# Mixture layers: the experts' sums added into x by accumulating transfers from GpSimd's queue

## The reference

```
x = w_norm * (xf * rsqrt(mean(xf * xf) + EPS))
probs = softmax(x @ w_router);  w_topk, sel = top_k(probs, 4)      # 32 experts, at most 128 tokens each
y = einsum('ecf,efh->ech', silu(g) * u, w_down)                    # per expert, on its tokens
out = zeros((T, H)).at[tok].add(gath * wv[:, None])                # each token: sum over its experts
sh = sigmoid(x @ w_shared_gate) * (silu(x @ sw_gate) * (x @ sw_up) @ sw_down)
return inp + out + sh
```

## Time and profile before

| what | us |
|---|---|
| median of three runs | 2876.78 |
| lowest and highest of the three | 2868.1, 2880.69 |
| profiled execution, whole | 2868.24 |
| its span, first to last instruction | 2866.5 |
| mean granted clock of TensorE | 0.955 of full speed |

### The profile page before, as it was taken

How to read it: one execution, slowest core, us unless ns; L and a number is a source line. 1 busy time by engine, 2 the same in 40 slices (tenths; PEclk the granted TensorE clock), 3 DMA queues, 4 the chain that set the end, 5 groups by cost and what they waited for, 6 DMA issues and landing times. The chain is left out here.

```text
span 2866.5 us, 39819 instructions
## 1 busy us (share of the span) xinstructions
PE 2626.2 (92%) x14164; PEld 1258.6 (44%) x14164; DVE 1950.7 (68%) x4228; ACT 1263.9 (44%) x1908; POOL 656.0 (23%) x640
## 2 busy tenths in 40 slices
PE   4988999999999999788898997899999999898998
PEld 2442233333333332344555564344445454455665
DVE  6778888887887886487675334867767676486334
ACT  2432466556655667543221221255555556421221
POOL 1454132131231300144001441212111110000442
PEclk8996899999999999999999998799999999999999
DMA  3004331303303210000401663723334430300566
GB/s 121 1 1 104 51 52 21 56 29 46 62 17 51 52 16 1 1 1 1 156 18 42 158 146 90 132 50 54 50 68 62 62 62 2 110 34 17 127 153 174
DMA packets 162592, 175.74 MB, mean 61 GB/s; under 512 B 19090, under 2 KB 135762, under 8 KB 162258
## 3 DMA queue, kind: packets, MB, share of 16 engines
q1 hardware_dynamic: 146948, 152.57, 24.3%
q0 software_dynamic: 12416, 17.84, 3.8%
q10 hardware_dynamic: 3040, 2.88, 0.4%
HBM read 116.32 MB, written 56.13 MB: 60 GB/s over the span
## 5 line engine op out<-in xcount | busy, mean ns | idle before, releaser
L1827 DVE TENSOR_REDUCE a_mx<-a_bank 128x1 f32<-128x512 f32 (+3 forms) x1792 | 1029.1, 627 | 274.2 <-PE a_bank L1564 186.2
L1700 ACT ACTIVATE a_E<-a_bank 128x1024 f32<-128x1024 f32 (+3 forms) x896 | 795.3, 931 | 462.4 <-PE a_bank L1621 317.9
L1564 PE MATMUL a_bank<-a_KT,a_QT 96*128 96x512 bf16 (+4 forms) x1792 | 596.3, 376 | 37.0 <-DVE a_mx L1827 27.4
L1621 PE MATMUL a_bank<-a_QT,a_KT 99*128 99x512 bf16 (+4 forms) x1792 | 508.3, 359 | 4.0 <-DMA a_QT<-a_mT 1.6
L1636 PE MATMUL a_bank<-a_E,a_Vg 128*32 128x512 f32 (+3 forms) x3584 | 438.6, 561 | 0.7 <-ACT a_E L1700 0.7
L1564 PEld LDWEIGHTS a_bank<-a_KT,a_QT 96*128 96x128 bf16 (+1 forms) x1792 | 152.6, 98 | 530.9 <-DVE a_mx L1827 331.1
L1621 PEld LDWEIGHTS a_bank<-a_QT,a_KT 99*128 99x128 bf16 (+1 forms) x1792 | 170.5, 99 | 176.5 <-ACT a_E L1700 35.2
L999 ACT ACTIVATE d_silu<-d_bank 128x512 f32<-128x512 f32 x96 | 57.2, 596 | 361.2 <-PE d_bank L873 357.5
L888 PE MATMUL d_bank<-wdT,d_hT 128*128 128x256 f32 (+1 forms) x768 | 196.9, 400 | 7.5 <-DVE d_hT L1088 7.5
L466 POOL TENSOR_TENSOR f_hl<-f_hT,f_hh 128x512 f16<-128x512 f32 x96 | 111.0, 1156 | 388.4 <-ACT f_hh L485 388.4
L792 POOL DMA_INDIRECT d_xg<-normalised,d_index x64 | 67.5, 1054 | 538.2 <-issue 535.1
(11 more groups left out here) (246 smaller groups left out, 3548.8 us busy)
## 6 DMA issues: line engine op xcount, KB each, us to landing
parts<-a_parts SPq DMA_DIRECT2D x64, 384.0 KB, 2.5
a_QT<-parts SPq DMA_DIRECT2D x180, 128.0 KB, 5.9
a_KT<-parts SPq DMA_DIRECT2D x180, 128.0 KB, 9.2
d_wgu<-in_L_ffn_w_gate SPq DMA_DIRECT2D x64, 176.0 KB
d_wgu<-in_L_ffn_w_up SPq DMA_DIRECT2D x64, 176.0 KB
d_wd<-in_L_ffn_w_down SPq DMA_DIRECT2D x64, 176.0 KB
normalised<-d_xn SPq DMA_DIRECT2D x8, 1152.0 KB, 4.7
acc<-d_zero SPq DMA_DIRECT2D x2, 4224.0 KB, 15.6
```

What stands on the lines that cost most here:

```text
L1564: last = nc.tensor.matmul(out[:, 0:w], QT[0:W, h, qt * P:(qt + 1) * P], KT[0:W, h, kh * HALF:kh * HALF + w], start=True, stop=not diag)
L1621: last = nc.tensor.matmul(out, KT[:, h, kt * P:(kt + 1) * P], QT[:, h, half * HALF + c0:(half + 1) * HALF], start=True, stop=not diag)
L1700: nc.scalar.activation(E[:, u % 2, 2 * pair:2 * pair + 2, c0:HALF], bank[:, 2 * pair:2 * pair + 2, c0:HALF], ACT.Exp).then_inc(exps, 1)
L1827: nc.vector.tensor_reduce(mx[:, j, qt, kh:kh + 1], out[:, 0:w], AX.X, ALU.max).then_inc(freed_dve, 1)
```

## The change

GpSimd takes over. After its wait for all expert additions it issues, for each chunk q, one direct transfer that reads the chunk's rows of `acc` and adds them into x in SBUF (`accum_op=ADD`). It waits for `x_done` of the chunk first, and from the fifth on for the transfer four before it, since four semaphores `summed` are used in turn. At the end it waits for all eight. SyncE's fetches and VectorE's additions are gone. In `d6_` SyncE stores chunk q when `summed` says so. In `d4_` VectorE takes the statistics of chunks 0 and 1 in slots (8, 1) and (8, 2), behind the residual of the slot. TensorE's and ScalarE's instructions are the same as before.

```diff
-    finishes = {slots[n]: qs for n, qs in ((len(slots) - 7, (0, 1)), (len(slots) - 6, (2,)), (len(slots) - 5, (3,)),
-                                           (len(slots) - 4, (4,)), (len(slots) - 3, (5,)), (len(slots) - 2, (6,)), (len(slots) - 1, (7,)))}
+    measured = {slots[len(slots) - 4 + q]: q for q in range(TPB // CT)}
...
-                sp.wait_ge(added, 16 * NE)
-                for q in range(ROWS):
-                    fetch(q)
-                for q in range(NCH):
-                    if final:
-                        sp.wait_ge(finished, START + q + 1)
+                if final:
+                    for q in range(NCH):
+                        sp.wait_ge(summed[q % SUMS], 16 * (q // SUMS + 1))
                         sp.dma_start(rows_of(dram["out"], q), core.x[:, q * CT:(q + 1) * CT, :]).then_inc(sent, 16)
-                    if q + ROWS < NCH:
-                        fetch(q + ROWS)
...
+                def sum_up(q):
+                    pool.wait_ge(x_done, START + (q + 1) * CT)
+                    if q >= SUMS:
+                        pool.wait_ge(summed[q % SUMS], 16 * (q // SUMS))
+                    nc.gpsimd.dma_start(core.x[:, q * CT:(q + 1) * CT, :], rows_of(acc, q), accum_op=ALU.add).then_inc(summed[q % SUMS], 16)
...
                 pool.wait_ge(added, 16 * NE)
+                for q in range(NCH):
+                    sum_up(q)
+                for q in range(SUMS):
+                    pool.wait_ge(summed[q], 16 * (NCH // SUMS))
...
-                def finish(q):
-
-                    tiles = core.x[:, q * CT:(q + 1) * CT, :]
-                    dve.wait_ge(back[q % ROWS], START + 16 * (q // ROWS + 1))
-                    dve.wait_ge(x_done, START + (q + 1) * CT)
-                    nc.vector.tensor_tensor(tiles, tiles, back_in[:, q % ROWS], ALU.add).then_inc(finished, 1)
-                    if q < TPB // CT and not final:
-                        dve.wait_ge(finished, START + q + 1)
-                        for i in range(CT):
-                            last = nc.vector.bn_stats(bn[:, q * CT + i, :], core.x[:, q * CT + i, :])
-                        last.then_inc(stats, 1)
+                def take_statistics(q):
+
+                    dve.wait_ge(summed[q % SUMS], 16 * (q // SUMS + 1))
+                    for i in range(CT):
+                        last = nc.vector.bn_stats(bn[:, q * CT + i, :], core.x[:, q * CT + i, :])
+                    last.then_inc(stats, 1)
...
-                    for q in finishes.get((c, j), ()):
-                        finish(q)
+                    if not final and (c, j) in measured:
+                        take_statistics(measured[(c, j)])
```

More of the change, by code:

```diff
@@ L624, in mixture_phase @@
     XG = 2 * DEEP
-    ROWS = 4
+    SUMS = 4
     STEPS = 17
@@ L699, in mixture_phase @@
         bn = sb(tag + "bn", [P, TPB, 6])
-        back_in = xn[:].rearrange("p s i d -> p (s i d)")[:, 0:ROWS * CT * D].rearrange("p (q i d) -> p q i d", q=ROWS, i=CT)
         bank = ps(tag + "bank", [P, 8, 512])
@@ L707, in mixture_phase @@
                  "masked ranked ranks_used pos_s chosen marked spotted tabled index_s gu silu_s silu2_s h_s down_s scaled x_done "
-                 "e_turned xgT_s e_gu_s e_silu_s e_silu2_s e_h_s h_turned hT_s dn_s y_s posted finished stats aggregated sent")
+                 "e_turned xgT_s e_gu_s e_silu_s e_silu2_s e_h_s h_turned hT_s dn_s y_s posted stats aggregated sent")
         (w_in, s_in, zeroed, root1, root2, scales, setup, cleared, normed, turned, xT_kept, logit_s, lg_kept, shifted, exp_s, gated, route,
          masked, ranked, ranks_used, pos_s, chosen, marked, spotted, tabled, index_s, gu_ready, silu_ready, silu2_s, h_ready, down_ready, scaled,
-         x_done, e_turned, xgT_s, e_gu_s, e_silu_s, e_silu2_s, e_h_s, h_turned, hT_s, dn_s, y_s, posted, finished, stats, aggregated,
+         x_done, e_turned, xgT_s, e_gu_s, e_silu_s, e_silu2_s, e_h_s, h_turned, hT_s, dn_s, y_s, posted, stats, aggregated,
          sent) = (sem(tag + n) for n in names.split())
         xn_sent = [sem(f"{tag}xn_sent{s}") for s in range(2)]
-        back = [sem(f"{tag}back{s}") for s in range(ROWS)]
+        summed = [sem(f"{tag}summed{q}", 0) for q in range(SUMS)]
         w_slot = [sem(f"{tag}w_slot{s}") for s in range(DEEP)]
@@ L718, in mixture_phase, with rows_of @@
         ident = core.const("ident")
+        def rows_of(tensor, q):
+            return tensor[q * CW:(q + 1) * CW, :].rearrange("(i p) d -> p i d", p=P)
         nc.all_engine_barrier()
@@ L752, in weights @@
                     sp.dma_start(wd[:, s], dram["L1_ffn_w_down"][e].rearrange("(h f) d -> f h d", h=2)).then_inc(w_slot[s], 16)
[L754 to L762, removed]
                 sp.wait_ge(cleared, START + 1)
```

## The result

| kernel | median of five, us | range | profiled execution: span, us |
|---|---|---|---|
| before | 2876.78 | 2868.1 to 2882.37 | 2866.5 |
| changed | 2897.26 | 2893.8 to 2903.44 | 2895.4 |

The ratio is 1.0075, with a 95% interval from 1.005 to 1.010: 14 to 29 us slower. The forecast was 2899 us.

The account below looks back on a forecast made before the run. The last phase was taken as bound by TensorE and the DMA engines at nearly the same moment, the first mixture as held up by VectorE. +5 and +17 us on the 2876.8 us median gave 2899 us, range 2882 to 2922.

Parts of the forecast that it names:

- VectorE and TensorE: First mixture: hidden work starts 3.1 us earlier, the clock gives 2.47 us more, x is done 5.6 us earlier.
- The price of a sum: Each 524 kB accumulating transfer takes 3.28 us at 160 GB/s, bounds 1.37 and 4.7 us.
- The rule that I had set behind the trace: A reducing transfer reads two sources at half rate: 2.7 us per transfer, about 9 us less in all.
- Who binds the first phase: First mixture: eight transfers back to back, 26.2 us, land at 1770.3; the backlog decides, x alone would allow 1768.8.
- The drain: End of both mixture phases: GpSimd's drain loses its cover and takes 5.3 us after the last landing.
- The first barrier: End of the first mixture: it opens at 1775.7 in place of 1770.7, +5 us.
- The last phase: Stores and sums share the engines, 37.2 us of work; the span ends at about 2883.4, +17 us.
- second rival, overlap: Last phase: stores go beside the additions, so +7.6 there and +12 to +13 in all, 2889 us; chance 14%.
- The drain counted from the last issue: Ends of both mixtures: the drain counts 7.7 us from the last issue's end, +1.8 and +15, 2894 us; chance 20%.
- Copy rate: Both mixtures: 1.37 us a transfer and no drain toll, so x decides; 1.4 us faster, 2875 us; chance 6%.
- Slow transfers: Both mixtures: 4.7 us a transfer, each end 11.4 us later again; +45, 2922 us; chance 13%.
- an issue that grows with the rows: Both mixtures: 6.2 us per issue makes GpSimd the bound, about +29 and +33, 2939 us; chance 5%.

Follow-up runs that it names:

- kernel with later additions: Kernel before with only one VectorE addition ahead of the first mixture's last hidden tile, other additions and statistics later; two timings, ratios 0.9983 and 0.9984.
- late-drain kernel: Kernel before with one wait more: GpSimd waits until x is done before it drains, in each mixture phase; no transfer added; 2881.96 us.
- run with one store: Changed kernel with seven of the last phase's eight stores left out, only chunk 7 stored; 2883.42 us.
- two phases run alone: Kernel before with the change in one mixture phase only: first phase 2881.36 us, ratio 1.0024; last phase 2885.96 us, ratio 1.0039.
- plain kernel: Changed kernel with plain transfers from GpSimd's queue in place of accumulating ones, which changes what is computed; 2879.85 us.

## Why the prediction came out right, and where its steps did not

**VectorE and TensorE.** Right. The forecast was a wait of 2.3 us, 12.0 us of matmuls and x done 5.6 us earlier; measured were 2.12, 12.00 and 5.2. How much the old order costs varies between runs, with the 13.95 to 16.49 us of its matmuls. The kernel with later additions shows that this part needs only the order.

**The price of a sum.** Wrong for a queue of sums: 3.28 us forecast, 524 / 196 = 2.67 measured. I had taken the rate in the middle of one short burst, 160 GB/s, for the steady one. A transfer that runs alone does move at that rate: the last of the first phase, 154 GB/s over the 3.4 us from 1772.8 to 1776.2, with a DMA share of 1.02. With another transfer queued behind, the share is 1.23, so the packets' times overlap, and the rate is 193 to 196 GB/s; a burst alone could not show that. The rule that I had set behind the trace (the Trainium skill, Collectives: The Full Stack, "The bandwidth ceiling: the fold count and why AG ≠ RS ≠ AR"), two reads at half the copy rate, gives 2.7 us as an estimate, and the runs come near it: against the steady mix of fetches and stores the factor is 384 / 196 = 1.96, against the plain transfers of the same queue 355 / 196 = 1.8, and 355 / 209 = 1.7 where both have packets of 4 kB. I let a row that was near in kind, but had no second transfer behind it, decide against that price. What the prediction gave as its worth, about 9 us less in all, was wrong by its own steps: at 2.7 us x and not the backlog would have bound the first phase, and the total would have been 2.1 us (1770.3 - 1768.2) and 4.3 us (8 x 0.54), or 6.4 us, less.

**Who binds the first phase.** Wrong in the mechanism, and close in the number. The forecast had eight transfers back to back and the last landing 32.4 us after the last expert addition's issue; it landed after 31.8. At 2.67 us the engines are through with seven sums at about the time x is done, the last transfer is issued only then, and they stand nearly idle (share 0.07 from 1771 to 1773) until its data come. Alone it took 5.8 us to land, near the 2.0 + 3.3 + 0.3 = 5.6 that I had for that case; 0.6 us more pass before GpSimd drains, where I had 0.1.

**The drain.** Right in kind, and the late-drain kernel shows it without any other edit: with its cover gone it stands in front of the barrier. The size was off by a fifth, 4.22 us in place of 5.28. That 4.22 goes with direct transfers of 1 kB rows behind the indirect ones, plain or adding, and 5.93 with 4 kB rows, is what the runs show, not why.

**The first barrier.** Forecast +5, measured +3.7: the last landing 0.7 us earlier, 0.5 us more between it and the drain, and a drain 1.1 us shorter.

**The last phase.** Right in the mechanism, +17 forecast, +13.3 measured: the last store's issue came 2.7 us earlier than forecast and the drain was 1.1 us shorter. The sum of the works was the right form (the second rival, overlap, falls by the run with one store). Its terms were off in opposite ways: sums 0.6 us too dear each, 4.9 in all, and the mix with stores 0.4 us too cheap each, 2.8 in all. The last store was issued 38.7 us after the last expert addition's issue, forecast 41.4. The prediction read a little too much into rows 4: 355 GB/s over 22 us are 7.8 MB, or 15 transfers of 524 kB and not 16; nothing was added up from that. The drain and the last store end within 0.4 us of each other, so neither alone is the end; in the forecast the drain led by 2 us.

**The total.** Forecast +22, measured +20.5 by the medians, but only 17.0 by the two stretches and 18.1 by the two phases run alone. The median of before that I built on was the same with five runs. That the forecast met the median within 2 us is thus partly luck: its ends were 5 us too dear, and the profile does not say where the last 3.5 us of the median come from. They are within its interval.

**The rivals.** The drain counted from the last issue: fallen by the late-drain kernel. Overlap: fallen. Copy rate: the plain kernel is that case, and it shows what it would have been worth with the drain in place, first stretch 34.3 and last 34.8, still 6 us over before. Slow transfers, and an issue that grows with the rows, have fallen too: a sum took 2.67 us and not 4.7, and the issue of 512 rows took 1.28 us, less than the 1.55 of 128 indirect ones.

## What to carry to other kernels

When work moves onto a transfer, follow its last piece to the end of the phase: a VectorE addition of 1.2 us behind the last result became an issue, a transfer and a landing of 5.8 us, 0.6 us more until GpSimd went on, and the drain of the queue that issues it came on top because nothing was left to hide it. When the DMA engines are full at the end (share near 1 in the windows), mind that here an addition in a transfer took 1.7 to 1.8 times as long as the same transfer without it, and what VectorE was relieved of was no gain there. A price read from a transfer that runs alone is not that of a queue of them: here 3.3 us against 2.67. And before moving work away from an engine that holds up another, try it behind the one instruction that is waited for; here that alone gave the whole gain.

## What the runs showed of the hardware

- Additions into SBUF from GpSimd's queue, 524 kB each with rows of 1 kB, ran at 193 to 196 GB/s with a DMA share of 1.23 when queued one behind the other, at 209 with rows of 4 kB; one alone at 154. The same transfers without the addition ran at 355. One alone landed 5.7 to 5.9 us after the start of its issue, without the addition 4.1; where GpSimd waited for it, its drain began 0.6 us later.
- Additions with plain stores beside them moved 236 GB/s in all.
- GpSimd's drain in a phase that used its queue took 5.28 us after indirect transfers, whether it began at once or 26 us after the last landing, 4.14 to 4.22 us where direct ones came behind them, 5.93 with direct ones of 4 kB rows. Begun before the landing it lasted until 3.0 us past it, in both phases.
- TensorE's 48 matmuls after a wait of 5.18 us took 13.95, 14.47 and 16.49 us in three runs, with a granted clock of 0.50 for part of them; after a wait of 2.12 us in the first mixture 12.00 in all nine runs. In the last phase they took 13.59 to 15.28 us in four of the kernels, at waits of 2.12 and 2.32 us, and there too the clock was at 0.50 for part of the matmuls (0.64 over the first four us of the 13.64, 0.50 over four us of the 15.28); what brings it down there stays open.
